# Attention tables built by ScalarE and VectorE straight from x1, and the first batch of each early group moved to the end of its slot

## The reference

```python
o1 = matmul((adj == 1), matmul(V, w1))       # adj holds 0 or 1 here; the terms for 2 and 3 are empty
x = layernorm(x + o1 + o2 + o3 + bias)       # x1
h = x @ W.T + b
e = (h @ we1 + be1) + (h @ we2 + be2).T
e = where(e >= 0, e, 0.01 * e)
scores = where(adj > 0, e, -9e15)
x = layernorm(x + softmax(scores, axis=1) @ h)
```

## Time and profile before

| | us |
|---|---|
| median of three runs | 1557.63 (1556.46 to 1559.41) |
| the profiled execution | 1559.72 |
| its span | 1558.1 |
| TensorE matmuls busy | 1422.6 (91%) |
| VectorE busy | 1092.0 (70%) |
| ScalarE busy | 978.1 (63%) |
| GpSimd busy | 116.1 (7%) |

### The profile page before, as it was taken

How to read it: one execution, slowest core, us unless ns; L and a number is a source line. 1 busy time by engine, 2 the same in 40 slices (tenths; PEclk the granted TensorE clock), 3 DMA queues, 4 the chain that set the end, 5 groups by cost and what they waited for, 6 DMA issues and landing times. The chain is left out here.

```text
span 1558.1 us, 19404 instructions
## 1 busy us (share of the span) xinstructions
PE 1422.6 (91%) x6934; PEld 670.4 (43%) x6934; DVE 1092.0 (70%) x2432; ACT 978.1 (63%) x1534; POOL 116.1 (7%) x154
## 2 busy tenths in 40 slices
PE   0867697989999999999999987999999999999996
PEld 0433243444444444444444433444444444444443
DVE  3677667877877868768778657576667676666663
ACT  1333526457457556456456559787888788788873
POOL 2111011100110100100100021000000000000000
PEclk9999799999999999999999997999999999999998
DMA  9999999993979979967969311000000000100100
GB/s 133 138 126 116 126 110 119 128 114 49 117 96 99 106 69 123 83 68 96 84 67 119 28 62 47 8 28 28 28 28 28 28 28 28 55 28 28 35 1 15
DMA packets 87684, 109.60 MB, mean 70 GB/s; under 512 B 4960, under 2 KB 71072, under 8 KB 87584
## 3 DMA queue, kind: packets, MB, share of 16 engines
q0 software_dynamic: 67584, 67.12, 47.1%
q1 hardware_dynamic: 20000, 41.20, 8.0%
HBM read 296.49 MB, written 13.14 MB: 199 GB/s over the span
## 5 line engine op out<-in xcount | busy, mean ns | idle before, releaser
L1222 PE MATMUL ps<-pos_masks,tables 128*128 128x512 fp8e4 x2048 | 616.4, 383 | 39.2 <-DVE pos_masks L607 32.1
L1004 ACT ACTIVATE neg_masks<-e_row,cols 128x512 int8<-128x512 f32 x816 | 509.7, 708 | 110.9 <-PE ps L1222 46.3
L1222 PE MATMUL ps<-neg_masks,tables 128*128 128x512 fp8e4 x1632 | 492.1, 383 | 0.0
L1180 PE MATMUL ps<-edge_masks,tables 128*128 128x512 fp8e4 (+1 forms) x2048 | 464.1, 385 | 0.0
L1222 PEld LDWEIGHTS ps<-pos_masks,tables 128*128 128x128 f16 x2048 | 200.4, 99 | 285.9 <-issue 49.5
L1180 PEld LDWEIGHTS ps<-edge_masks,tables 128*128 128x128 f16 x2048 | 201.4, 99 | 233.3 <-issue 13.7
L1222 PEld LDWEIGHTS ps<-neg_masks,tables 128*128 128x128 f16 x1632 | 161.3, 99 | 197.7 <-issue 9.0
L605 DVE TENSOR_TENSOR neg_masks<-pos_masks,neg_masks 128x2048 uint16<-128x2048 uint16 x102 | 125.0, 1225 | 91.4 <-ACT neg_masks L1004 88.3
L589 DVE TENSOR_SCALAR edge_masks<-edges 128x512 uint16<-128x512 uint16 x512 | 123.4, 306 | 78.1 <-PE ps L1180 78.1
L589 DVE TENSOR_SCALAR pos_masks<-edges 128x512 uint16<-128x512 uint16 x512 | 114.2, 285 | 88.4 <-PE ps L1222 88.4
L992 ACT ACTIVATE edges<-ps 128x1024 uint8<-128x1024 bf16 x64 | 65.1, 1017 | 172.5 <-PE ps L1189 172.5
(11 more groups left out here) (133 smaller groups left out, 845.0 us busy)
## 6 DMA issues: line engine op xcount, KB each, us to landing
adj_in<-adj POOLq DMA_DIRECT2D x84, 512.0 KB, 12.2
tables<-adj POOLq DMA_DIRECT2D x28, 512.0 KB, 31.2
e_row<-e_scratch SPq DMA_DIRECT2D x34, 256.0 KB, 3.9
edges<-adj POOLq DMA_DIRECT2D x16, 512.0 KB, 11.9
part_scratch<-a_c_rows SPq DMA_DIRECT2D x18, 256.0 KB, 2.5
part_in<-part_scratch SPq DMA_DIRECT2D x18, 256.0 KB, 3.0
edges<-x SPq DMA_DIRECT2D x8, 512.0 KB, 6.6
x_rows<-x SPq DMA_DIRECT2D x8, 512.0 KB, 5.5
```

Of the source, the lines that this page charges most:

```text
L1004: ins = e.activation(gate_bufs[GATE[m]][:, n:n + GR].bitcast(I8), e1row[:, q % 2, :], ACT.Sign, bias=t2[:, JC * c + j:JC * c + j + 1])
L1180: ins = e.matmul(ps[:, h, :], v_hl[:, i, JC * c + j, :], U0[:, n:n + GR].bitcast(kind), start=c == 0 and j == 0 and i == 0, stop=c == NCH ...
L1222: ins = e.matmul(z_bank(q, k), tab[:, c, 2 * k + i, j, :], mask[:, n:n + GR].bitcast(F8A), start=first and j == 0 and i == 0, stop=final a ...
```

## The change

Tables are made straight from x1: ScalarE writes each of the 8 rows' f16 high part with b or d as scale (columns 0 to 126), and the last column from b or d; VectorE computes source times factor minus high part in one operation per row. The f32 products, the column of ones and all of GpSimd's part in the tables go. `table_source` gives x1, or for tables 4 to 6 the block read again. The sums of x1's rows take 127 columns, the last is set to 64 at the start. Tables 0 to 3 are made at off 4 (high) and off 4 or 5 (low), tables 4 to 7 by ScalarE at the end of slots 66, 67, 68, 68 and by VectorE at the end of the slot behind. Waits on the products go: y, x1, the next x rows and the third gate buffer no longer wait for a table's low part or wait for it alone.

In the slot of a fresh batch TensorE runs the batch behind the transposes, and VectorE makes its masks behind the edge masks, ahead of low and rows_sum.

```diff
-AGAIN = (K, K + 1, K + 2)
+AGAIN = (4, 5, 6)
+BUILD = {4: K + 2, 5: K + 3, 6: K + 4, 7: K + 4}

# SP
             def next_rows(S):
                 e.wait_ge(s_er, S + 1)
-                ge(e, s_lo, min(S + 1, 4))
                 xg_load(S + 1)

# GpSimd
-            def ones_column(S):
-                e.wait_ge(s_x1st, 16 * (S + 1))
-                e.wait_ge(s_er, S + 1)
-                e.memset(X1[:, :, D - 1:D], 1.0).then_inc(s_one, 1)
...
-            def table_products_again(n):
-                e.wait_ge(s_xr[n], 16)
-                ge(e, s_lo, 4 + n)
-                e.memset(xr[n][:, :, D - 1:D], 1.0).then_inc(s_one2, 1)
-                e.wait_ge(s_one2, n + 1)
-                e.tensor_tensor(xr_b, xr[n], factor(bq, n + 4), ALU.mult).then_inc(s_pt2, 1)
-                e.wait_ge(s_pt2, 2 * n + 1)
-                e.tensor_tensor(xr[n], xr[n], factor(dq, n + 4), ALU.mult).then_inc(s_pt2, 1)

# VectorE
-            def low(S, pb, pd):
-                for k, src in ((0, pb), (2, pd)):
+            def low(S):
+
+                src = table_source(S)
+                for k, f in ((0, bq), (2, dq)):
                     e.wait_ge(s_hi, 2 * S + k // 2 + 1)
-                    ins = e.tensor_tensor(tab[:, S, k + 1], src, tab[:, S, k], ALU.subtract)
+                    for t in range(RB):
+                        j = JC * S + t
+                        e.scalar_tensor_tensor(tab[:, S, k + 1, t, 0:D - 1], src[:, t, 0:D - 1], f[:, j:j + 1],
+                                               tab[:, S, k, t, 0:D - 1], ALU.mult, ALU.subtract)
+                    ins = e.tensor_tensor(tab[:, S, k + 1, :, D - 1], f[:, JC * S:JC * (S + 1)],
+                                          tab[:, S, k, :, D - 1], ALU.subtract)
                 ins.then_inc(s_lo, 1)
...
                 for m in at(k):
-                    masks(m)
-                    after(m)
-                for S, off in tails(k):
-                    if off == 5 and (S < 4 or S == NS - 1):
-                        low(S, yT8, xg[:, :, :])
-                for n, slot in enumerate(AGAIN):
-                    if k == slot + 2:
-                        low(4 + n, xr_b, xr[n])
+                    if not fresh(m):
+                        masks(m)
+                        after(m)
...
                 if 1 <= k <= K:
                     edge_masks(k - 1, 1)
+                for m in at(k):
+                    if fresh(m):
+                        masks(m)
+                        after(m)
...
+                    if off == 4 + min(S, 1) and S < 4:
+                        low(S)
                     if off == 5:
                         rows_sum(S)
+                for S in BUILD:
+                    if k == BUILD[S] + 1:
+                        low(S)

# ScalarE
-            def table_products(S):
...
-            def high(S, pb, pd):
...
+            def high(S):
+
+                if S in (2, 3):
+                    e.wait_ge(s_pk, GUEST[S] + 1)
+                if S in AGAIN:
+                    e.wait_ge(s_xr[S - 4], 16)
+                    e.wait_ge(s_l0, 2 * K)
+                else:
+                    e.wait_ge(s_x1, S + 1)
                 e.wait_ge(s_bd, 2 * (S + 1))
+                src = table_source(S)
+                for k, f in ((0, bq), (2, dq)):
                     for t in range(RB):
+                        j = JC * S + t
+                        e.activation(tab[:, S, k, t, 0:D - 1], src[:, t, 0:D - 1], ACT.Copy, scale=f[:, j:j + 1])
+                    e.activation(tab[:, S, k, :, D - 1], f[:, JC * S:JC * (S + 1)], ACT.Copy).then_inc(s_hi, 1)
...
-                    if off == 4 and (S < 4 or S == NS - 1):
-                        table_products(S)
+                    if off == 4 and S < 4:
+                        high(S)
+                for S in BUILD:
+                    if k == BUILD[S]:
+                        high(S)

# TensorE
                 for m in at(k):
-                    batch(m)
-                    after(m)
+                    if not fresh(m):
+                        batch(m)
+                        after(m)
                 if k < K:
                     turn(k)
+                for m in at(k):
+                    if fresh(m):
+                        batch(m)
+                        after(m)
```

More of the change, by code:

```diff
@@ L115, in at, with fresh @@
     return [m for m in range(NB) if SLOTS[m] == k]
+def fresh(m):
+    return SLOTS[m] == NCH * (BATCH[m][1] // 2 + 1) + START
 def ended(m):
@@ L271, in build @@
             "x1_stored", "e_products", "e_sums", "e1_ready", "e1_turned", "e1_turned_copied", "e1_stored", "b_d_ready")
-        s_one, s_pt, s_hi, s_lo, s_hp, s_ha = sems(
-            "ones_column", "table_products", "table_high", "tables_ready", "h_part", "h_rows_added")
+        s_hi, s_lo, s_hp, s_ha = sems("table_high", "tables_ready", "h_part", "h_rows_added")
         s_half = sem("packed_4_half")
         s_t2c = sem("t2_bounded")
-        s_one2, s_pt2 = sems("ones_column_again", "table_products_again")
         s_xr = [sem(f"x1_again_{n}") for n in range(3)]
@@ L317, in group_rows, with table_source @@
             return block_rows(a, g // 2)[:, GT * (g % 2):GT * (g % 2 + 1), :]
+        def table_source(S):
+            return xr[S - 4] if S in AGAIN else X1
         def all_stored(e):
@@ L503, in _ @@
                                 pattern=[[-1, P]], channel_multiplier=1).then_inc(s_ident, 1)
-            def ones_column(S):
-                e.wait_ge(s_x1st, 16 * (S + 1))
-                e.wait_ge(s_er, S + 1)
-                e.memset(X1[:, :, D - 1:D], 1.0).then_inc(s_one, 1)
-            def factor(t, S):
-                return t[:, JC * S:JC * (S + 1)].unsqueeze(2).broadcast_to([P, RB, D])
-            def table_products_again(n):
-                e.wait_ge(s_xr[n], 16)
-                ge(e, s_lo, 4 + n)
-                e.memset(xr[n][:, :, D - 1:D], 1.0).then_inc(s_one2, 1)
-                e.wait_ge(s_one2, n + 1)
-                e.tensor_tensor(xr_b, xr[n], factor(bq, n + 4), ALU.mult).then_inc(s_pt2, 1)
-                e.wait_ge(s_pt2, 2 * n + 1)
-                e.tensor_tensor(xr[n], xr[n], factor(dq, n + 4), ALU.mult).then_inc(s_pt2, 1)
-            for k in range(K + 6):
-                for n, slot in enumerate(AGAIN):
-                    if k == slot:
-                        table_products_again(n)
+            for k in range(K):
                 loads(k)
-                for S, off in tails(k):
-                    if off == 3:
-                        ones_column(S)
             e.wait_ge(s_top, 1)
@@ L554, in _ @@
             e.memset(onesq, 1.0).then_inc(s_const, 1)
-            e.memset(hacc, 0.0).then_inc(s_const, 1)
+            e.memset(hacc[:, 0:D - 1], 0.0).then_inc(s_const, 1)
+            e.memset(hacc[:, D - 1:D], float(JB)).then_inc(s_const, 1)
             def split_rest(v):
@@ L702, in quotients @@
                     e.wait_ge(s_hwc, 1)
-                    e.wait_ge(s_lo, NS - 1)
+                    e.wait_ge(s_lo, NS)
                 for h in range(2):
@@ L998, in gates @@
                 if GATE[m] == 2:
-                    e.wait_ge(s_lo, NS)
+                    e.wait_ge(s_er, NS)
                 e.wait_ge(s_row[q % 2], 16 * (q // 2 + 1))
@@ L1011, in y_of @@
                     e.wait_ge(s_l0, 2 * (NCH * S + NCH - 1) + h + 1)
-                    ge(e, s_lo, min(S, 4))
                     ge(e, s_er, S)
@@ L1022, in x1_of @@
                 ge(e, s_ha, S)
-                ge(e, s_pt, 2 * min(S, 4))
+                ge(e, s_lo, min(S, 4))
                 ge(e, s_x1st, 16 * S)
@@ L1085, in after @@
                         out_of(q - LOWS)
-            def fresh(m):
-                return SLOTS[m] == NCH * (BATCH[m][1] // 2 + 1) + START
             e.wait_ge(s_const, 1)
@@ L1103, in _ @@
                         b_d_of(S)
-                    if off == 5 and (S < 4 or S == NS - 1):
-                        high(S, yT8, xg[:, :, :])
-                for n, slot in enumerate(AGAIN):
-                    if k == slot + 2:
-                        e.wait_ge(s_l0, 2 * K)
-                        high(4 + n, xr_b, xr[n])
                 for m in at(k + 1):
```

25 lines of the change are left out of this document (5 added, 20 removed).

## The result

The changed kernel takes 1599.93 us (median of 4 runs, 1591.5 to 1602.1), the kernel before in the same job 1558.52 us (4 runs, 1556.46 to 1560.19): 1.0256 times as long, 95% interval 1.0216 to 1.0296. It is slower by 41.4 us; the forecast said 43. The profiled execution took 1602.1 us, 42.4 more than that of before.

What follows compares the result with a forecast made beforehand. The span was taken as TensorE's matmul time (1422.6 of 1558.1 us) plus about 135 us of gaps. Terms 17.7 + 16.4 - 4 + 13 = 43 us on the 1557.6 us median gave 1601 us, range 1578 to 1614 with rival 1.

Steps and rivals of the forecast that it cites:

- slot 13: First fresh slot: second e1 row's DMA goes out earlier, so gates, transposes and batch 0 come earlier; -4 us.
- slot 21: Fresh slot: bf16 copy stands behind both sets of gates on ScalarE, so transposes and batch run late; 5.7 us.
- slot 29: Fresh slot with the same ScalarE queue of gates ahead of the bf16 copy; 5.6 us lost.
- slot 37: Fresh slot with almost no wait before, taken as nearer to the later slots; 5.1 us lost.
- slots 45, 53, 61: Late fresh slots: batch waits for masks behind edge masks that wait for layer 0; 3 x (4.2 + 1.7) = 17.7 us.
- late tables: Last four tables: longer ScalarE and VectorE work in short, filled slots delays batch 49; +13 us.
- The clock's term: Behind each new gap in slots 45, 53 and 61, TensorE's clock partly drops to 1.2 GHz; 1.7 us each.
- Rival 1: Clock doesn't fall in the new gaps and the low parts are short; 27 us slower, 1585 us, chance 0.22.
- rival 2: Reorder costs nothing because VectorE has the masks ready; only the tables' 13 us remain, 1571 us, chance 0.07.
- Tables 0 to 3 off the path: Early tables: VectorE's 2.3 us more per low part fits in over 5 us to spare; nothing on the path.
- Rivals 3 and 4: 3: ready masks shrink waits of slots 13 to 37, 1541 us, chance 0.05; 4: both parts cancel, 1558 us, 0.02.

Runs made afterwards that it cites:

- e5: Changed kernel with ScalarE's exponentials of the rows ahead of the late high parts in slots 66 to 68; same instructions up to slot 65; 1591.91 us.
- e1: Changed kernel with the order of before for fresh batches (batch ahead of transposes, masks at the top of VectorE's slot), tables staying changed; 1568.55 us.
- e3: Changed kernel with VectorE's masks of a fresh batch moved ahead of the edge masks, TensorE's order staying changed; 1581.74 us.
- e4: Changed kernel with the load of the next x rows waiting again for the table's low part; 1603.17 us.
- e7: Kernel before with direct tables for S = 0 to 3 only; old order and last four tables as before; 1558.85 us, ratio 0.999.
- e8: Kernel before with only the late stretch reordered (low parts, high parts, exponentials, table 7's row sums); 1554.4 us.
- e2: Kernel before with only the fresh batches and their masks moved to the new order, tables as before; 1620.03 us, ratio 1.0387.
- e9: e7 with e8's late moves, and the low parts of tables 2 and 3 a slot later; 1550.69 us.

## Why the prediction held

| step | forecast | measured | e5's execution |
|---|---|---|---|
| slot 13 | -4 | -5.2 | -6.7 |
| slot 21 | +5.7 | +3.7 | +5.5 |
| slot 25 | none | +2.3 | -0.9 |
| slot 29 | +5.6 | +4.6 | +4.7 |
| slot 37 | +5.1 | +6.1 | +4.3 |
| slots 45, 53, 61 | 17.7 | 20.4 | 18.7 |
| late tables | +13 | +10.1 | other kernel |
| rest | 0 | +0.2 | |
| sum | 43 | 42.1 | |

The path and the waits are the forecast ones. That the sum came out within 1 us is in part luck: the terms are off by 1 to 3 us either way and cancel, and another execution of the same instructions moves single terms by as much.

- **Fresh slots late (45 to 61).** The mechanism is the forecast one, shown by e1 (no gap with the old order) and e3 (no wait for masks with the masks ahead of the edge masks). The waits come to 3.8 or 3.9 us in each of the three slots, where 3.9 was forecast. The clock's term was too small for this execution: 1.7 us per gap, taken from the mean 0.79 of the earlier trace rows, against 9.5 - 6.9 = 2.6 us and a mean of 0.61. In e5's execution the same gap at slot 53 cost 8.6 - 6.9 = 1.7 us, at a mean of 0.79. Rival 1, in which the clock stays up, is refuted by the same windows, rival 2 by e1 and e3.
- **Slots 21 and 29.** ScalarE's queue ran as written down: the bf16 copy ends at 268.53, 273.8 on the time scale of before (shift -5.2), forecast 274.6. The batch lost less clock than put in: it and the transposes run from 268.58 to 277.27, 8.7 us, where 7.35 is full speed, so 1.3 us lost where 2.2 were forecast. Behind waits of 9.16 and 9.25 us at the same slot e5 lost 1.7 us and e4 2.6. That ScalarE's order makes these waits is read from the trace; no run moves the copy ahead of the gates.
- **Slot 13.** Both DMAs go out behind the first row's, the gates start at 170.71 with no wait, and the transposes start at 176.77, forecast 176.8. e4 gives 3.6 us to the lifted wait.
- **Slot 25 has no term.** The prediction names no gap there, though the transposes of slot 25 already waited 5.19 us in the kernel before. SP's DMA, ScalarE's gates and TensorE's transposes there in the changed kernel:
```profile
321.92 0.39 SPq L388 DMA_DIRECT2D e_row<-e_scratch  x1
...
328.82 5.00 ACT L1001 ACTIVATE neg_masks<-e_row,cols 128x512 int8<-128x512 f32 x8 [14.06 <-issue]
...
334.88 1.04 PE L1176 MATMUL ps<-idb,packed_bf 128*128 128x128 bf16 x8 [7.48 <-ACT packed_bf L980]
```
The e1 row is issued 1.6 us earlier than before (323.50), as all else there, but it takes 6.8 us to land and not 4.5. The gates start at once when it is there, and TensorE waits 7.48 us instead of 5.19. In e5's execution the row took 3.6 us and TensorE waited 4.26. So the 2.3 us are the time of one small load, which differs from execution to execution; they can't be put down to the change.
- **Tables 0 to 3 off the path:** shown by e7, 0.999 [0.9973, 1.0007].
- **Late tables.** A low part takes 4.35 us (997.34 to 1001.69; forecast 4.7), a high part 4.9 (5.2). Freed of the 31.8 us that the fresh slots had added, the exponentials end at 961.5 (before 957.8, forecast +6, measured +3.7), and from there it is 16.3 us to batch 49 (forecast 17.0). The gap of batch 46 closed, and batch 47 starts at 946.9, 0.4 us later than before (forecast 2). e5 bears out the part of the exponentials and e7 the sum; the part of the low parts is read from the trace. The removal of GpSimd's products did free VectorE: the product of 2.92 us in the earlier trace rows takes 1.22 here, and still 2.92 in e8, which keeps GpSimd's products.
- **The rule of the Trainium skill** ("VectorE: DVE Perf Modes", the TRN2 errata) gave an estimated 3.1 us per low part. Measured are 4.35 us, 0.27 us for each scalar_tensor_tensor of 127: here the spacing in the trace decides, and going by the row was right.
- **Rivals 3 and 4** fell: e1 against the changed kernel shows that the order takes 31 us instead of giving 12, and the result itself, 41.4 us slower, leaves no room for two parts that cancel.

In short, and taken in this order: the late tables cost 9.7 us (e1 against e7) and the early ones nothing (e7), and on top of them the order costs 31.4 us (e1). The prices hold only in this order, since on the tables of before the same order costs 60 us (e2).

## What to carry to other kernels

Moving work behind a step pays only if all that it needs is ready by then: look for what the producer itself waits for (here edge masks that wait for layer 0's buffer), because the orders of several queues hang together. Where a gain upstream vanishes at one fixed place, look at the in-order queue that feeds that place: here a small row load behind a store of results was worth 15 us, and the early tables nothing. Replacing another engine's work by many small instructions was free where a slot had slack, and cost 10 us in the stretch where each slot was already filled. Before a loss of 1 to 3 us at one place is explained, it should be seen in a second execution of the same instructions.

## What the runs showed of the hardware

- What the clock takes behind one and the same gap differs between executions. Behind 3.76 us ahead of the batch of slot 53 it was 2.6 us in the changed kernel (granted clock 0.61 over 8 us) and 1.7 in e5 (0.79 over 8 us). Behind some 9.2 us ahead of the transposes of slot 21 it was 1.3 us in the changed kernel, 1.7 in e5 and 2.6 in e4. By what it is set these runs don't show.
- The load of an e1 row (256 KB) took 4.5 us from issue to landing at slot 25 of the kernel before, 6.8 in the changed kernel, 3.6 in e5 and 9.2 in e9, beside the adj loads. The longest seen was 11.0 us (e4, issued at 276.31). A margin for such a load has to hold the longest.
- The second of two products of 128x1024 in f32 on VectorE took 2.92 us beside GpSimd's products (kernel before and e8) and 1.22 us without them (changed kernel).
